# Who issues the zeroing of an aggregation table: from ScalarE's queue to the end of SyncE's load list

## The reference, cut to what matters

```python
x = _layernorm(x + _L0_gnn_ref(x, node_vec1, edge_attr_16, edge_attr_4, src, dst, ...), axis=-1)
x = _layernorm(x + _L1_gnn_ref(x, edge_attr_16, edge_attr_4, ..., edge_index), axis=-1)
x = _layernorm(x + _L2_gnn_ref(x, edge_attr_4, edge_attr_8, ..., edge_index), axis=-1)
x = _layernorm(x + _L3_gnn_ref(x, node_vec1, edge_attr_4, edge_attr_8, ..., src, dst, 16), axis=-1)
```

## Time and profile before

| what | us |
|---|---|
| median of 3 runs | 4392.32 |
| lowest, highest | 4391.31, 4588.6 |
| the profiled execution, its time | 4397.57 |
| its span | 4395.8 |
| edge phase of layer 0, first to last scatter issue (L564) | 139.7 to 694.8 |

### The profile page before, as it was taken

How to read it: one execution, slowest core, us unless ns; L and a number is a source line. 1 busy time by engine, 2 the same in 40 slices (tenths; PEclk the granted TensorE clock), 3 DMA queues, 4 the chain that set the end, 5 groups by cost and what they waited for, 6 DMA issues and landing times. The chain is left out here.

```text
span 4395.8 us, 72815 instructions
## 1 busy us (share of the span) xinstructions
PE 3382.7 (77%) x13920; PEld 1659.6 (38%) x13920; DVE 3296.0 (75%) x8785; ACT 2472.2 (56%) x7452; POOL 3185.6 (72%) x3110
## 2 busy tenths in 40 slices
PE   0888887995999999999930088887997888886676
PEld 0333334662444434444410033332665333334554
DVE  1677767994888888888868746564999556658999
ACT  0333335995555555555537745554999444435777
POOL 1577777996788888888636667775787677766887
PEclk9898898997999999999965589998999899988998
DMA  9322226995455455555459923232998222226786
GB/s 382 116 75 76 74 77 211 318 317 136 117 128 130 120 132 121 128 129 120 115 168 371 355 73 82 81 82 75 317 326 281 73 78 78 77 69 205 240 241 201
DMA packets 582482, 713.96 MB, mean 162 GB/s; under 512 B 77680, under 2 KB 407734, under 8 KB 582130
## 3 DMA queue, kind: packets, MB, share of 16 engines
q1 hardware_dynamic: 491446, 533.50, 40.6%
q0 software_dynamic: 84672, 141.06, 12.0%
q10 hardware_dynamic: 6268, 38.40, 2.1%
HBM read 484.47 MB, written 244.35 MB: 166 GB/s over the span
## 5 line engine op out<-in xcount | busy, mean ns | idle before, releaser
L564 POOL DMA_INDIRECT aggregates<-agg_out,scatter_index x588 | 589.9, 1003 | 324.4 <-issue 183.0
L1329 ACT ACTIVATE y_chunk<-residual,ln_minus_mean_rstd,ln_rstd 128x160 f32<-128x160 f32 x1568 | 700.9, 548 | 76.0 <-DMA x_layer<-y_chunk 55.5
L1398 POOL TENSOR_TENSOR ln_rstd<-ln_var_eps,minus_half 128x4 f32<-128x4 f32 x392 | 497.5, 1269 | 108.6 <-ACT ln_var_eps L1338 73.1
L552 POOL DMA_INDIRECT gathered<-x_layer,gather_index x392 | 394.2, 1006 | 132.0 <-issue 114.2
L1293 PE MATMUL psum<-self_weights,x_chunk_T 128*128 128x160 f32 (+1 forms) x2352 | 429.2, 328 | 58.1 <-ACT x_chunk_T L1352 54.3
L644 PE MATMUL psum<-identity,scaled_x 128*128 128x128 f32 x588 | 152.8, 296 | 384.4 <-ACT scaled_x L598 359.2
L1504 DVE BATCH_NORM_STATS2 ln_stats<-residual 128x6 f32<-128x160 f32 x1568 | 396.2, 309 | 6.8
L709 DVE COPY gather_index<-src_index 128x4 int32 (+1 forms) x147 | 25.4, 173 | 496.4 <-DMA gathered<-x_layer,gather_index 372.8
L1293 PEld LDWEIGHTS psum<-self_weights,x_chunk_T 128*128 128x128 f32 x2352 | 359.7, 197 | 94.1 <-ACT x_chunk_T L1352 53.4
L552 POOL DMA_INDIRECT gathered<-in_x,gather_index x196 | 212.8, 1086 | 153.1 <-ACT scaled_x L598 63.2
L880 POOL DMA_INDIRECT aggregates<-agg_out,last_index x196 | 234.5, 1196 | 114.5 <-issue 62.8
(11 more groups left out here) (231 smaller groups left out, 10449.4 us busy)
## 6 DMA issues: line engine op xcount, KB each, us to landing
x_layer<-y_chunk SPq DMA_DIRECT2D x294, 320.0 KB, 4.7
x_chunk<-x_layer SPq DMA_DIRECT2D x294, 320.0 KB, 4.6
agg_chunk<-aggregates SPq DMA_DIRECT2D x196, 320.0 KB, 5.4
sh_rows<-in_sh_big SPq DMA_DIRECT2D x49, 768.0 KB, 8.5
agg_chunk<-aggregates SPq DMA_DIRECT2D x98, 384.0 KB, 5.7
aggregates<-zero_rows ACTq DMA_DIRECT2D x1, 36864.0 KB
x_chunk<-in_x SPq DMA_DIRECT2D x98, 322.0 KB, 3.8
agg_chunk<-aggregates SPq DMA_DIRECT2D x98, 322.0 KB, 3.8
```

What stands on the lines that cost most here:

```text
L552: eng.indirect_dma_start(gathered[:, par, b, 0:width], None, x_table[l][:, :], bass.IndirectOffsetOnAxis(idx_src[:, par, b:b + 1], 0))\
L564: eng.indirect_dma_start(agg_table[:, :], bass.IndirectOffsetOnAxis(idx_last[:, q, b:b + 1], 0), agg_out[:, q, b, :], None, bounds_check=N ...
L1329: op = eng.activation(y_out[:, buf, b, :], res[:, buf, b, :], ACT.Identity, bias=shift[:, buf, b:b + 1], scale=rstd[:, buf, b:b + 1])
L1398: eng.tensor_tensor(rstd[:, buf, :], var_eps[:, q, :], minus_half[:, 0:T], ALU.pow)\
```

## The change

The two zeroing DMAs, with the wait for the zero rows, go from ACT's queue to SP's, behind everything in `setup_sync` and ahead of layer 0's edge steps. Two waits (for the segment flags and for the copied weights) are dropped. ACT begins with layer 0's edge steps. The sizes of the DMAs and the semaphore that the first scatter waits for stay.

```diff
-        def setup_scalar(eng):
+        def zero_table(eng):
 
             eng.wait_ge(P["zeroed"], 1)
-            eng.wait_ge(P["rows_in1"], 16)
-            eng.wait_ge(P["again_in"], 16 * (2 * len(CONV) + 3))
             flat = zeros[:, :, :].rearrange("p j c -> p (j c)")
             many = N // (8 * TILE)
             eng.dma_start(agg_table[0:8 * TILE * many, :].rearrange("(p k j) c -> p k (j c)", k=many, j=8),
...
         @block.sync
         def _(eng):
             setup_sync(eng)
+            zero_table(eng)
             for l in range(layers):
...
         @block.scalar
         def _(eng):
-            setup_scalar(eng)
             for l in range(layers):
```

## The result

Over 20 runs each, the changed kernel took 4413.99 us (median) against 4389.81 us. The ratio of the fast runs, which leaves out one slow run of the kernel before (4588.6 us), is 1.0047, 95% interval 1.0036 to 1.0059. That is slower by 20.6 us, interval 15.8 to 25.9 us; the two medians as they stand are 24.2 us apart. The forecast was +15.7 us and 4408.0 us; the time lies in its range and the direction is as forecast.

The account below looks back on a forecast made before the run. No engine bounds the whole kernel; the zeroed table ends layer 0's prologue. Later table +13.2 us (14.8 less 1.6) plus restart 2.5 gave +15.7 on 4392.3, so 4408.0 us; own range 4400 to 4416, wider 4397 to 4432.

Parts of the forecast that it names:

- What bounds: End of layer 0's prologue: set by the zeroed table at 139.4 us or so, hiding ACT's stall by 8.5 us.
- The start: SP's list ahead of the zeroing: it ends at 43.1 us, so the zeroing starts 14.8 us later.
- Rival A: SP's issues stay slow (1.26 us) without the bulk beside them; zeroing starts at 66.7 us, 4431.6 us; chance 0.10.
- Less beside it: Bulk zeroing: 0.68 MB of SP's loads and group 0's gathers now move ahead of it, 1.6 us less.
- X: End of the prologue, when the zeroed table is ready: 139.4 us before, forecast to move +13.2 us to 152.6.
- The restart: PE and POOL after X: group 2's edge rows queue behind the zeroing on SP, costing +2.5 us, bounds 0 and +6.
- B: SP's queue: group 2's edge rows pass the bulk, so only X counts: +13.2, 4405.5 us; chance 0.09.
- C: Layer 0's loop: POOL catches up by 1.2 us a group, the +15.7 us are gone, 4392 us; chance 0.08.
- D: SP's queue: something unseen makes it dearer by a lot, over 4480 us; chance 0.03.
- A sign of being wrong that came up: Last scatter of layer 0: forecast wrong if its shift is not the first scatter's plus 0 to 6 us.

Follow-up runs that it names:

- the last three versions without a delay: Kernel before, small zeroing DMA first from 16 partitions: 0.9996; that without two waits: 0.9976; waiting for weights alone, two tail DMAs first: 0.9983.

## Why the prediction was right

*What bounds.* The claim that the table, not ACT, ends the prologue held. Freeing ACT with the start unchanged gained nothing (with a table 5.8 us late), and delaying the start on ACT's own queue cost at least as much as the change by the medians.

*The start.* Forecast 43.1 us, measured 44.34. The list itself stood 0.3 us later in this execution, the 12 issues of L405 took 0.49 us each where I took 0.45, and L396 and L398 a little over 0.58. Rival A, the slow pace, is out: the pace of SP's issues depended on the bulk beside it.

*Less beside it.* Forecast 1.6 us; from the issue to the first scatter it is 109.0 us (153.36 - 44.34) against 111.4, so 2.4 us less. Both errors nearly cancel, which is luck: X was put at +13.2, and the first scatter is at +13.65.

*The restart.* Forecast +2.5 us, measured 12.8 - 10.4 = +2.4, and removed alone by moving one pair of DMAs. Its make-up was a bit off. I put PE's L656 of group 2 behind the whole tail, at X + 1.5. It ran 0.24 us before the first scatter, because 98 of the 112 packets of the rows moved beside the tail and not after it. Against that, the way from there to group 1's `agg_out` took 12.1 us (153.12 to 165.24) where I had taken the 10.6 of before. PE's restart was slow in its first 5 us: L654 takes 1.22 us, where L656 of group 2 had taken 0.69. The granted clock in the changed kernel is 1.00 up to 73 us, 4 us after PE's last matmul before the stall, then 0.50, the 1.2 GHz level, until 158.5 us; matmuls of one form (16x512 or 64x512) take 1.05 to 1.22 us before that and 0.59 to 0.69 after it. Standing alone does not bring it: in the kernel before PE stood from 68 to 104 us at 1.00.

*The rivals.* B (the edge rows pass the bulk) is refuted by PE's wait of 83.95 us, though most of the rows did pass the tail. The trace now shows the order for SP's queue too: issued by 134.05 + 1.18 us, the rows moved only behind the bulk, 98 packets beside the tail and 14 behind it, and PE used them at 153.12. The Trainium skill, "DMA: Bandwidth & Descriptors", section "Queues, rings and completion order", has the order for each DMA engine's ring by itself, and not for the queue as a whole. The trace agrees: 98 packets moved some 12 us ahead of the 14. C (POOL catches up) is refuted by 20 runs: +15.8 us at least. D did not happen. One detail of the held SP I had not priced: the edge rows' own issue was held another 12.64 us. It cost nothing, since it was over at 135.23 us and the bulk in front of the rows moved until past 138.

*A sign of being wrong that came up.* I had written that the forecast is wrong if the shift at the last scatter is not the one at the first plus 0 to 6 us. It is 12.4 us, below the 13.65 of the first scatter and the 16.1 of the second set. One pair of profiles cannot use that sign, as phases of this length differ by more than that between executions; it neither supports the forecast nor, by itself, C.

*What is not accounted for.* The sum at the second set of scatters is +16.1 us and the time +20.6 (15.8 to 25.9). The shift lies just inside the interval. Up to some 10 us could come from elsewhere; the runs cannot separate this from chance, and it stays open.

## What to carry to other kernels

Ask of a long stall which wait behind it ends last: 76 us of ScalarE cost nothing here because GpSimd's first scatter had to wait for the same transfer until later. When a big transfer gates a phase, what counts is when it starts and how it ends (a remainder written by two of 16 DMA engines was 14 us); who issues it is second, unless the issuer's next DMA is something that the phase needs at once. And if two DMAs go out back to back on a compute engine's queue, the second one's issue waits for the first, so the small one first frees the engine. That does not make the transfer ready earlier: with the small one on two engines the first scatter was 5.8 us later, and only with its rows spread over all engines, as in the last three versions without a delay, was it earlier.

## What the runs showed that I had not expected

- A DMA issued behind a bulk one on the same queue holds its issuer far beyond the second zeroing DMA: 12.64 us for the edge rows in the changed kernel, 16.02 us for three small loads in the run with the zeroing early on SP. There the list behind the bulk became the bound, and the phase lost 15 us although its table was earlier.
- A DMA queued behind a bulk one is not behind all of it: 98 of the 112 packets of the edge rows moved right behind the bulk, some 12 us before the tail was through.
- A tail spread on all engines is not free if its runs are short: 0.65 MB in 768 B runs took some 7 us, at the end as at the start. The version with runs of 6,144 and 3,840 B, which starts 16.5 us later than the earliest one, had its table 1.4 us before it; that longer runs alone did this is not shown.
- Starting the zeroing 26.7 us earlier (2.15 instead of 28.87 us, with the same two DMAs) brought the table 5.5 us earlier: SP's prologue loads share the DMA engines and its issues slowed, for three loads of L360 to 7.95 us from 1.29.
- The same kernel took 4390 us in the result's runs and 4746 to 4801 on the three chips of the experiments. The two profiles of it have a granted clock of 0.91 and 0.83 in the first edge phase, while the first 150 us agree within 1 us. Whether the clock is the cause was not tested.
